# A four-layer attention network on one core: nine planned merges of its stages replaced by one written table of turns

## What is computed

```python
xn = _layernorm(x)
s = _Lk_attn_ref(xn, ...)          # softmax attention, projections before and after
g = _silu(_Lk_ffn_ref(xn, ...))    # layer 0: SwiGLU; 1: Sinkhorn mixing; 2, 3: routed LoRA
x = x + s * g
```

```python
u = -jax.nn.logsumexp(Z + v[..., None, :], axis=-1)
v = -jax.nn.logsumexp(Z + u[..., :, None], axis=-2)
```

## Time and profile before

| what | value |
|---|---|
| median of 3 executions | 1445.67 us (1438.63 to 1447.93) |
| profiled execution: its time | 1444.44 us |
| profiled execution: its span, first to last instruction | 1442.7 us |
| mean granted clock of TensorE | 0.871 |
| busy: PE / DVE / ACT / POOL | 76% / 60% / 40% / 22% of the span |

### The profile page before, as it was taken

How to read it: one execution, slowest core, us unless ns; L and a number is a source line. 1 busy time by engine, 2 the same in 40 slices (tenths; PEclk the granted TensorE clock), 3 DMA queues, 4 the chain that set the end, 5 groups by cost and what they waited for, 6 DMA issues and landing times.

```text
span 1442.7 us, 20140 instructions
## 1 busy us (share of the span) xinstructions
PE 1098.7 (76%) x7480; PEld 446.7 (31%) x7480; DVE 871.4 (60%) x1777; ACT 578.9 (40%) x801; POOL 320.4 (22%) x514
## 2 busy tenths in 40 slices
PE   2889998977788568648437367878788988898887
PEld 1434443433233223314213012312222233333333
DVE  4222221005667589885898887657667587736663
ACT  2433332003554423145114146574445555434452
POOL 1145542017722101011011053700100031111220
PEclk9889999996999678768678588988789999999999
DMA  7322210012100002001101021401012111211100
GB/s 278 118 66 66 69 62 0 0 45 85 46 21 18 7 18 66 12 1 51 33 17 52 24 68 43 131 17 39 17 32 63 51 42 31 70 47 30 52 17 30
DMA packets 54901, 69.74 MB, mean 48 GB/s; under 512 B 9526, under 2 KB 43444, under 8 KB 54800
## 3 DMA queue, kind: packets, MB, share of 16 engines
q1 hardware_dynamic: 50828, 58.58, 12.9%
q0 software_dynamic: 3984, 9.98, 2.3%
HBM read 49.45 MB, written 18.82 MB: 47 GB/s over the span
## 4 chain that ended last, share of the span: by engine, by line
PE 36%; DVE 31%; ACT 5%; issue 4%; SPq 1%; DMA 1%; ACTq 0%; DVEq 0%
DVE w_mx L1404 13%; PE w_banks L669 10%; PE w_po L1319 9%; PE w_banks L1301 4%; PE w_banks L1273 4%; DVE w_region L1891 3%; PE w_banks L1261 2%; ACT w_pr L1347 2%; DVE w_region L1888 2%; DVE w_region L1869 2%; DVE w_region L1886 2%; PE w_banks L1329 2%; PE w_banks L1555 2%; DVE w_region L1884 1%; DVE w_region L1882 1%
## 5 line engine op out<-in xcount | busy, mean ns | idle before, releaser
L1404 DVE TENSOR_REDUCE w_mx<-w_banks 128x2 f32<-128x1024 f32 (+3 forms) x352 | 376.8, 1086 | 195.7 <-PE w_banks L1273 191.4
L1347 ACT ACTIVATE w_pr<-w_banks 128x1024 f32<-128x1024 f32 (+1 forms) x312 | 315.0, 1013 | 429.6 <-PE w_banks L1301 428.3
L1386 POOL TENSOR_SCALAR_AFFINE_SELECT w_pr<-w_pr 128x512 f32<-128x512 f32 (+1 forms) x184 | 104.6, 569 | 561.1 <-ACT w_pr L1347 561.0
L1301 PE MATMUL w_banks<-w_qs,w_ks 49*128 49x512 f16 (+7 forms) x832 | 136.7, 353 | 89.9 <-DVE w_mx L1404 58.8
L1273 PE MATMUL w_banks<-w_ks,w_qs 48*128 48x512 f16 (+7 forms) x832 | 145.0, 361 | 40.5 <-DVE w_mx L1404 23.3
L1319 PE MATMUL w_po<-w_pr,w_vz 128*17 128x512 f32 (+7 forms) x1152 | 154.2, 561 | 12.7 <-ACT w_ou L1369 12.7
L78 PE MATMUL f_pp<-xt,sl_region 128*128 128x512 f16 x672 | 148.9, 382 | 3.5 <-POOL sl_region L508 3.5
L1261 PE MATMUL w_banks<-mask_half,ident_half 64*128 64x128 bf16 (+1 forms) x768 | 67.3, 255 | 37.8 <-DMA w_ks<-stack_scratch 17.1
L482 DVE TENSOR_TENSOR sl_region<-sl_region,f_pp 128x512 f32<-128x512 f32 x28 | 19.2, 687 | 121.1 <-ACT sl_region L497 121.1
L78 PEld LDWEIGHTS f_pp<-xt,sl_region 128*128 128x128 f16 x672 | 65.1, 98 | 84.6 <-issue 5.3
L1301 PEld LDWEIGHTS w_banks<-w_qs,w_ks 49*128 49x128 f16 (+1 forms) x832 | 41.7, 98 | 138.5 <-issue 57.5
(11 more groups left out here) (222 smaller groups left out, 1513.9 us busy)
## 6 DMA issues: line engine op xcount, KB each, us to landing
stack_scratch<-sl_region SPq DMA_DIRECT2D x102, 128.0 KB
w_qs<-stack_scratch SPq DMA_DIRECT2D x96, 96.0 KB, 2.4
sl_region<-in_L_gu SPq DMA_DIRECT2D x14, 512.0 KB
w_stage<-in_L_w POOLq DMA_DIRECT2D x36, 128.0 KB, 2.4
sl_region<-in_L_down SPq DMA_DIRECT2D x14, 256.0 KB
stack_scratch<-p_qk SPq DMA_DIRECT2D x24, 128.0 KB
w_ks<-stack_scratch SPq DMA_DIRECT2D x32, 96.0 KB, 2.6
bw_stage<-in_L_w SPq DMA_DIRECT2D x4, 640.0 KB, 11.8
```

The costliest lines, as they stand in the source:

```text
L1301: mm = pe.matmul(g.banks.pair_at(f)[:, half, at:at + T - q0], g.ks[base:base + self.rows + 1, k_slot, k_place, j * P:(j + 1) * P], g.qs[ba ...
L1347: act.activation(g.probs.at(self.pr_fill[s])[:, :, 0:width], g.banks.pair_at(self.s_fill[s])[:, :, 0:width], ACT.Exp, scale=self.a.scale). ...
L1386: pool.affine_select(out=diagonal, in_=diagonal, compare_op=ALU.is_ge, fill=0.0, base=0, pattern=pattern, channel_multiplier=-1).then_inc( ...
L1404: dve.tensor_reduce(out, g.banks.pair_at(self.m_fill[m])[:, :, 0:heads * keys].rearrange("q h (p k) -> q h p k", k=keys), AX.X, ALU.max).t ...
```

## The change

The nine calls of `merge` are gone. All ticks form seven strands, each a fixed sequence, and one call at the end takes them in the turns that a table of letters and counts writes down: `a` the attention bodies, `b` the chains of Outward, Normalise, Project and lead, `s` both Streams, `r` the Routed stages, `w` all weight splits, `c` the lead of a01, `l` the first small loads. The planner of before is replaced by a loop that takes the turns and stops the build if a tick would come before one that it needs. No stage's code changes, so all engines issue the same instructions on the same data; their order changes, and with it the banks, and for some fills the waits. The number of table loads on ScalarE is 32 in both.

```diff
-def merge(strands, order, emitted, banks):
...
+TURNS = """
+    w6 a w5 a5 l a12 w a w a2 w6 a w a w a3 w a4 w a w a w a w a w a6 c w c a2 c w c2 a c a2 c w a c2 w a w a c a w c w
...
+def merge(strands, turns, order, emitted, banks):
...
+    for turn in turns.split():
+        letter, count = turn[0], int(turn[1:] or 1)
+        for stage, t in flat[letter][at[letter]:at[letter] + count]:
...
             banks.now = stage, t
...
+            stage.plan(t)
+            order.append((stage, t))
+            emitted[stage, t] = len(emitted)
+        at[letter] += count
...
-        cut = s0.bal_at + 180
-        merge([[body_of(a01)], [all_of(o00), all_of(n10), all_of(p10), lead_of(a10)], [some_of(s0, 0, cut)]], order, emitted, g.banks)
...
-        cut1 = s1.bal_at + 60
...
-        merge([[body_of(a11)], [all_of(o10), all_of(n20), all_of(p20), lead_of(a20)],
-               [some_of(s1, cut1, s1.ticks[-1] + 1)], [all_of(split2)]],
-              order, emitted, g.banks)
...
+        strands = {"l": [all_of(small)], "w": [all_of(x) for x in (split1, split2, split3, split_base, split4)],
+                   "a": [all_of(a00)] + [body_of(x) for x in (a01, a10, a11, a20, a21, a30, a31)],
...
+                   "s": [all_of(s0), all_of(s1)], "r": [all_of(x) for x in (r20, r21, r30, r31)]}
+        merge(strands, TURNS, order, emitted, g.banks)
```

More of the change, by code:

```diff
@@ L1892, in balance @@
         op.then_inc(self.balanced.sem, 1)
-def merge(strands, order, emitted, banks):
-    flat = [[(stage, t) for stage, ticks in strand for t in ticks] for strand in strands]
-    total = [sum(stage.cost(t) for stage, t in strand) for strand in flat]
-    at, spent = [0] * len(flat), [0.0] * len(flat)
-    def ready(k):
-        stage, t = flat[k][at[k]]
-        wanted = list(stage.needs(t))
-        if t == stage.ticks[0]:
-            wanted += stage.begins_after
-        return all(need in emitted for need in wanted)
-    while any(at[k] < len(flat[k]) for k in range(len(flat))):
-        waiting = [k for k in range(len(flat)) if at[k] < len(flat[k]) and ready(k)]
-        waiting.sort(key=lambda k: (spent[k] + flat[k][at[k]][0].cost(flat[k][at[k]][1]) / 2) / total[k])
-        for k in waiting:
-            stage, t = flat[k][at[k]]
-            users, fills = list(banks.users), len(banks.fills)
-            banks.now = stage, t
-            try:
-                stage.plan(t)
-            except Full:
-                banks.users[:], banks.fills[fills:] = users, []
-                continue
-            break
-        else:
-            raise RuntimeError("no tick can come next")
-        order.append((stage, t))
-        emitted[stage, t] = len(emitted)
-        at[k] += 1
-        spent[k] += stage.cost(t)
@@ new lines @@
+"""
+def merge(strands, turns, order, emitted, banks):
+    flat = {letter: [(stage, t) for stage, ticks in strand for t in ticks] for letter, strand in strands.items()}
+    at = dict.fromkeys(flat, 0)
+    for turn in turns.split():
+        letter, count = turn[0], int(turn[1:] or 1)
+        for stage, t in flat[letter][at[letter]:at[letter] + count]:
+            wanted = list(stage.needs(t))
+            if t == stage.ticks[0]:
+                wanted += stage.begins_after
+            if t > stage.ticks[0]:
+                wanted.append((stage, t - 1))
+            if not all(need in emitted for need in wanted):
+                raise RuntimeError("a tick comes too early")
+            banks.now = stage, t
+            stage.plan(t)
+            order.append((stage, t))
+            emitted[stage, t] = len(emitted)
+        at[letter] += count
+    if any(at[letter] != len(flat[letter]) for letter in flat):
+        raise RuntimeError("ticks are left over")
@@ L1939, in body_of @@
     return stage, range(0, stage.ticks[-1] + 1)
-def some_of(stage, first, last):
-    return stage, range(first, last)
 class Shared:
@@ L2118, in weave @@
                        + split_rows("L1_wo", wo1, 2) + split_rows("L1_w24", w24) + [(ins["L1_wb"], wb[:, 0], wb[:, 1])])
-        merge([[all_of(small), all_of(a00)], [all_of(split1), lead_of(a01)]], order, emitted, g.banks)
         o00 = Outward(g, h[0], 0, lambda part, c: wo[:, part, c, :], o_rows[:, 0, :], att(0), sl[:, 0], done(a00), None,
@@ L2137, in weave @@
         s1.begins_after = [(n11, n11.ticks[-1])]
-        cut1 = s1.bal_at + 60
-        merge([[body_of(a10)], [all_of(o01), all_of(n11), all_of(p11), lead_of(a11)],
-               [some_of(s0, cut, s0.ticks[-1] + 1), some_of(s1, 0, cut1)]], order, emitted, g.banks)
         o10 = Outward(g, h[1], 0, lambda part, c: wo1[:, part, c, :], o_rows[:, 1, :], att(0), sl[:, 0], done(a10),
@@ L2161, in weave @@
                        [(p11.made, len(p11.chunks)), (p11.v_made, p11.v_units), s1.ready(), (o01.made, NI)])
-        merge([[body_of(a20)], [all_of(o11), all_of(n21), all_of(p21), all_of(r20), lead_of(a21)], [all_of(split3)]],
-              order, emitted, g.banks)
         rows3 = Loads(g, "third", [(g.cos, ins["cos"]), (g.sin, ins["sin"]),
@@ L2191, in weave @@
         r30.begins_after = [(o21, o21.ticks[-1])]
-        merge([[body_of(a30)], [all_of(o21), all_of(n31), all_of(p31), lead_of(a31)], [all_of(split4), all_of(r30)]],
-              order, emitted, g.banks)
         store = out.rearrange("b (i p) d -> p (b i) d", p=P)
```

29 lines of the change are left out of this document (25 added, 4 removed).

## The result

The changed kernel takes 1346.2 us (median of 4 runs, 1344.2 to 1348.3) against 1445.4 (4 runs, 1438.6 to 1447.9): a ratio of 0.9321, 95% interval 0.9286 to 0.9356.

The account below looks back on a forecast made before the run. No engine was full overall; the bound changed by stretch, VectorE in the fourth (95%), TensorE leading from the sixth. Terms 1 + 7 + 0 + 12 + 6.6 + 2.5 = 29 us took 1444.4 to 1415 (median 1416), range 1390 to 1430.

Parts of the forecast that it names:

- Start, predicted 1 us: First stretch: operands load 5.1 us earlier but the first mask comes later, at 343.0; gain 1 us.
- Second and third, 7 + 0: Ten a01 ticks move beside s0, gain 7 us; third stretch's VectorE work within 1 us, gain 0.
- Fourth, 32 less: a11's stretch: s1 work leaves a full VectorE, so the stretch shrinks by 32 us.
- Fifth, 20 more: a20's stretch takes s1's moved work: parts of 73 and 92 us, 165 against 145, a loss of 20.
- the prediction's own signs: Expected stretch times: fourth near 97 us, a20's first 31 ticks 73, from o11 to a20's end 92.
- Table loads, nothing: Fifth stretch: three more ScalarE table loads at 1.28 us, 4 us in all, covered by idle time and costed at nothing.
- Sixth to eighth, 6.6: Work only exchanged between neighbours; p30's denser order brings the sixth to 88% TensorE, gain 6.6 us.
- End, 2.5: o31's first ticks go ahead of r31's Silu, removing TensorE's 2.75 us gap; gain 2.5 us.
- A: Fifth stretch: the chain from o11 starts late and keeps its 127 us pace, time 1468; chance 0.08.
- B: Fifth stretch: s1 costs its full price, 181 us, so no net gain, time 1445; chance 0.16.
- C: Second to fifth stretch: VectorE stays dense at 92%, 497 against 560 us, time 1371; chance 0.14.
- my tests for "wrong": Wrong if o11 to a21's first maximum exceeds 103 us, a20's first part 85, or second and third lose their gain.

Follow-up runs that it names:

- a01_a10_even: Changed kernel with the second and third stretch (a01, a10) at an even pace, same ticks in each: 1379.5 us, 0.9551.
- s_moved: Kernel before, even pace kept in every merge, only the Sinkhorn strand cut as in the new table: 1439.6 us, 0.9977.
- sqrt_early: Changed kernel with the Sqrt tick of n10, n20, n30 and n31 each put ahead of the attention tick before it: 1353.5 us, 0.9379.
- shift_up: Changed kernel with each attention tick one place earlier, 557 ticks elsewhere: 1393.1 us, 0.9643.
- a21_shares: Kernel before, sixth window cut into four even-pace merges with the table's shares of a21 ticks: 1442.8 us, 0.9982.
- a21_row: Kernel before with only the sixth window (a21 and its neighbours) in the table's order: 1432.0 us, 0.991.
- inner_order: Kernel before, its nine windows with the same ticks, but each window's ticks in the table's order: 1404.9 us, 0.974.
- the nine exchanges: Changed kernel with single ticks put ahead of attention ticks, in two kernels: four Sqrt ticks, 1353.5 us; five first Project ticks, 1357.6 us.
- shift1: Changed kernel with each attention tick one place later where it may, 557 ticks elsewhere: 1393.7 us, 0.9655.

## Why the prediction was right in direction and wrong in size

*Start, predicted 1 us.* The time is met, 1 us (422 to 421), but it is not shown: the first stretch varies by 6 us between kernels in which it has the same order. The first mask starts at 342.85, forecast 343.0. Part of that is luck, as the woven part itself began 1.2 us later than before (317.20 against 316.03):

```profile
342.85 1.36 POOL L1386 TENSOR_SCALAR_AFFINE_SELECT w_pr<-w_pr 128x256 f32<-128x256 f32 x3
```

*Second and third, 7 + 0.* Wrong: 28. s0's first VectorE instruction comes 41 us after the attention's start instead of 73 (495.38 before), where I had 15 to 20 earlier:

```profile
461.84 0.17 DVE L1790 TENSOR_SCALAR w_region<-w_region 128x4 f32<-128x4 f32 x1 [1.16 <-ACT w_region L1753]
```

"VectorE's work is within 1 us of what it was; 0" took equal work for equal time. a01_a10_even gives the whole back (252 to 284).

*Fourth, 32 less.* Right: 34, and s_moved shows the move of s1 alone to be the cause (31). VectorE is as full as before: busy 84.3 of 93 us, and 5.5 more for its 184 balancing and mixing ticks at 0.03.

*Fifth, 20 more.* In stretches by TensorE it is 10 more. The first part takes 67 us with VectorE at 64 (forecast 73), the second 95 (forecast 92):

```profile
764.00:831.00 67.00, 41.40 (x255) 9.31 (x254) 64.47 (x164) 40.05 (x53) 0.00 (x0) 0.86 0.05 14
831.00:926.00 95.00, 73.47 (x484) 24.56 (x482) 70.41 (x120) 55.85 (x75) 48.12 (x87) 0.93 0.26 76
```

The form of the sum was right, and it was a sum for this table only. It was too long by 6 us in the first part. The durations of VectorE's 164 instructions there add up to about 73 us, as forecast, but many begin before the row of the one before them ends, and together they cover 64. The net of fourth and fifth is 24 against the forecast 12 (by the prediction's own signs, 97 + 73 + 92 against 127 + 152, it would have been 17: the sum had counted the fifth from VectorE's 837, the signs from TensorE's 829). At an even pace the same cuts cost 32 in the fifth (s_moved), and the net is about nothing. The clock of the first part was 0.86 and not 0.75.

*Table loads, nothing.* The fifth stretch has 7 instead of 5, two more where I had said three, but it is their place that has a price: with cover it is nothing, and a pair ahead of an Exp on which a bank hangs costs 3 to 4 us (sqrt_early, shift_up). The Exp starts 1.30 us after its load does (996.06 to 997.36 above). The Trainium skill ("ScalarE: Activation LUTs", What ACT_TABLE_LOAD costs) has 2.66 us for a switch with its drain; no row here shows the drain.

*Sixth to eighth, 6.6.* This is the step that failed: "work is exchanged between neighbours, not removed". The work is indeed the same, and the three stretches take 398 us instead of 439, 41 less. The one gain that I did see there, p30's denser row, is not where it comes from: with the table's shares alone the sixth wins 3 (a21_shares), with its order 22 (a21_row). I had read TensorE's 151 of 178 us, 85%, as nearly full. But 15 of these 151 were the low clock, as the changed kernel's 136 for the same products shows, and the holes were waits that an order can remove. My bound of 15 for the sixth was itself too small (23).

*End, 2.5.* Right by the boundary: 2 (23 to 21). TensorE's gap is gone, filled with products of r31 that used to stand ahead of a31's last values. From those last values to the end it takes 24.8 us in both kernels, so part of the gain is booked in the eighth stretch. TensorE now works on o31 from 1328.01 while the Silu runs.

```profile
1328.01 2.75 PE L669 MATMUL w_banks<-w_wo,w_ot 128*128 128x512 f16 x12
1328.94 1.91 ACT L1587 ACTIVATE sl_region<-sl_region 128x2048 f32<-128x2048 f32 x1 [1.15 <-DVE sl_region L1608]
```

*The rivals.* A is out: o11's first product starts at 831 and a21's first maximum at 914, 83 us, under the 103 that I had named. B is out in this table, and it is very nearly what s_moved did, 1440 against B's 1445. C was nearly right where it spoke: it gave 497 us for the second to fifth stretch, and they take 505 (421 to 926). It said nothing of the last four, where the other 43 us lie. I gave it 0.14, and none of my tests for "wrong" looked for a gain that was too large.

Of the 70 us that the forecast lacks, some 21 are in the second and third, 12 in the fourth and fifth and 34 in the sixth to eighth. The common fault is that I kept each stretch's density as the even pace had left it, as if its holes belonged to the work. They belonged to the order: VectorE's wait for maxima scores in the table of runs falls from 191 to 114 us as the order comes nearer to the table's, and the time falls with it, though not one for one (inner_order and a01_a10_even wait 141 and 142 us and take 1405 and 1380).

What stays open: which of the many single places carry the rest (the nine exchanges explain 18 of the 47 us that shift1 loses), how much of the whole is the clock's (roughly 4 to 9 of 22 us in the sixth stretch, elsewhere not tried), and why the whole is worth 58 us more than the move and inner_order apart, beyond the 17 at the seams. That a bank held too long is the link between the engines is read from the waits; the number of banks was not varied. Each order also has its banks handed out anew, and no run kept the banks while it changed the order.

## What to carry to other kernels

Where several strands share engines that serve their queues in order, the holes of a stretch are not a property of its work: before costing a new order at "density as before", ask how many of them end with a wait for another engine, and count those as possibly removable. An order that is written out by hand or found by search pays at the scale of single ticks, so it has to be redone whenever a duration or a strand changes; its coarse outline alone was worth a fifth of the gain here. Look first at ticks that hold a queue for long (a table switch, a first product with a late operand): they belong where that engine would wait anyway.

## What the runs showed that I had not expected

- Moving 557 of 1765 ticks by one place costs 47 us (3.5%) with no work added or taken away, in either direction.
- The mean granted clock changes with the order alone: 0.858 (s_moved), 0.871 (before), 0.886 (shift1), 0.909 (after) with the same products. Raising it from 0.71 to 0.91 in a piece by repeated products did not shorten the piece. The Trainium skill ("TensorE: Matmul & The Clock Gate", What's actually happening) has the array slow down when idle and return when busy; the trace agrees, but here that is more a sign of the waits than their cost.
- The move of s1 by itself is worth 3 us and the order inside the old windows 38, and the whole table 99. Some 17 of the rest lie at the seams between the old windows, where a Silu or the first ticks of the next chain stand a few places elsewhere.
